# Long cross attention: queries of the first batches beside tile 9 of the running attention, peaks of batch 0 as 24 half steps beside its tiles 13 to 18

## What is computed

```python
q = _rope(q, T_q)          # 16 heads of 8, from x after the layer norm
k = _rope(k, T_k)          # 1500 context tokens
attn = jnp.einsum('bhqd,bhkd->bhqk', q, k) * SCALE
attn = jax.nn.softmax(attn, axis=-1)
out = jnp.einsum('bhqk,bhkd->bhqd', attn, v)
return out @ Wo.T
```

## Time and profile before

| | us |
|---|---|
| median of 3 runs (1635.27 to 1635.96) | 1635.84 |
| the profiled execution | 1629.23 |
| its span | 1627.4 |
| TensorE busy | 1475.6 (91%) |
| VectorE busy | 1066.2 (66%) |
| ScalarE busy | 868.7 (53%) |
| GpSimd busy | 744.2 (46%) |

### The profile page before, as it was taken

How to read it: one execution, slowest core, us unless ns; L and a number is a source line. 1 busy time by engine, 2 the same in 40 slices (tenths; PEclk the granted TensorE clock), 3 DMA queues, 4 the chain that set the end, 5 groups by cost and what they waited for, 6 DMA issues and landing times.

```text
span 1627.4 us, 41073 instructions
## 1 busy us (share of the span) xinstructions
PE 1475.6 (91%) x17022; PEld 947.9 (58%) x17022; DVE 1066.2 (66%) x1723; ACT 868.7 (53%) x1783; POOL 744.2 (46%) x670
## 2 busy tenths in 40 slices
PE   7879999999999799857699999999999999889998
PEld 4557888765444466525466666666666666555554
DVE  6885555433342377686588888888888888634554
ACT  3432333345654233315577777777777777743333
POOL 6773111100000057767488777778777776000000
PEclk9879999989999799968899999999999999989999
DMA  4003000041210420245555555464654654403320
GB/s 120 2 1 107 2 2 2 2 128 45 78 39 13 86 60 23 45 98 103 128 129 130 120 125 130 121 132 118 135 127 124 125 130 110 111 1 93 68 57 14
DMA packets 62539, 129.54 MB, mean 80 GB/s; under 512 B 15793, under 2 KB 38066, under 8 KB 59186
## 3 DMA queue, kind: packets, MB, share of 16 engines
q1 hardware_dynamic: 62354, 126.92, 33.5%
HBM read 100.22 MB, written 26.67 MB: 78 GB/s over the span
## 4 chain that ended last, share of the span: by engine, by line
PE 33%; POOL 11%; ACT 8%; issue 2%; DVE 2%; DMA 1%; SPq 0%; ACTq 0%; POOLq 0%; DVEq 0%
PE ps L1724 7%; POOL ARENA L1928 7%; PE ps L865 7%; PE ps L1708 5%; POOL ARENA L1934 4%; PE ps L877 3%; PE ps L1671 3%; ACT ARENA L1878 3%; PE ps L1662 2%; ACT ARENA L1856 2%; PE ps L1685 2%; ACT ARENA L1869 1%; ACT ARENA L1862 1%; PE ps L1733 1%; DVE ARENA L1798 1%
## 5 line engine op out<-in xcount | busy, mean ns | idle before, releaser
L1798 DVE TENSOR_REDUCE ARENA<-ps 112x2 f32<-112x1000 f32 x384 | 456.7, 1198 | 118.0 <-PE ps L1685 115.1
L1878 ACT ACTIVATE ARENA<-ps 125x448 f32<-125x448 f32 x768 | 378.4, 549 | 127.9 <-PE ps L1708 127.0
L1928 POOL TENSOR_TENSOR ARENA<-ARENA 64x500 f32<-64x500 f32 x192 | 264.8, 1379 | 104.4 <-ACT ARENA L1856 85.9
L107 POOL TENSOR_TENSOR rs<-rs,mhalf 128x1 f32<-128x1 f32 x96 | 57.7, 602 | 363.5 <-DVE rs L102 363.2
L865 PE MATMUL ps<-XT,ARENA 128*128 128x448 f32 x544 | 219.9, 549 | 0.0
L1708 PEld LDWEIGHTS ps<-ARENA 64*125 64x125 bf16 x3072 | 122.5, 134 | 133.3 <-ACT ARENA L1878 70.3
L1708 PE MATMUL ps<-ARENA 64*125 64x112 bf16 x3072 | 168.9, 228 | 20.0 <-ACT ARENA L1878 18.8
L1724 PE MATMUL ps<-ARENA 125*17 125x112 f32 x6144 | 184.9, 260 | 0.0
L865 PEld LDWEIGHTS ps<-XT,ARENA 128*128 128x128 f32 x544 | 104.6, 194 | 99.1 <-issue 98.7
L877 PE MATMUL ps<-ARENA 128*128 128x448 f32 x400 | 161.6, 539 | 0.0
L1685 PE MATMUL ps<-ARENA 64*112 64x500 bf16 x768 | 152.7, 387 | 9.0 <-DVE ARENA L1798 8.9
(11 more groups left out here) (228 smaller groups left out, 2106.2 us busy)
## 6 DMA issues: line engine op xcount, KB each, us to landing
ARENA<-key_parts SPq DMA_DIRECT2D x192, 187.5 KB, 4.1
ARENA<-in_ctxT SPq DMA_DIRECT2D x96, 250.0 KB, 3.8
key_parts<-ARENA SPq DMA_DIRECT2D x64, 375.0 KB, 2.7
ARENA<-token_weights SPq DMA_DIRECT2D x32, 512.0 KB, 5.6
ARENA<-in_L_ffn_W SPq DMA_DIRECT2D x1, 2048.0 KB, 8.8
ARENA<-query_parts SPq DMA_DIRECT2D x6, 192.0 KB, 6.0
ARENA<-in_c_ones SPq DMA_DIRECT2D x2, 562.5 KB, 14.7
ARENA<-in_L_attn_a SPq DMA_DIRECT2D x2, 512.0 KB, 5.3
```

Of the source, the lines that this page charges most:

```text
L1798: e.tensor_reduce(mxp[0:112, b % 2, 2 * g:2 * g + 2, ch], ps[0:112, b1:b1 + 2, 0:500], AX, ALU.max) \
L1878: e.activation(Pb[0:KT, n % NP_, 448 * h:448 * h + 448], ps[0:KT, b1[h], 0:448], ACT.Exp, bias=0.0, scale=1.0).then_inc(exped.sem, 1)
L1928: e.tensor_tensor(T2[r:r + 64, :], T0[64 - r:128 - r, n % 2, :], sin[64 - r:128 - r, sl], ALU.mult) \
```

## The change

Five things are changed.

1. Query 0 moves from tile 17 to tile 9, queries 1 and 2 from 18 and 19 to 17 and 18. They stand at the end of a tile, behind `output`. Query 0 uses bank 2 for both of its products, one after the other; each of the two matmuls now has its own signal.
2. The masks of batches 0, 1 and 2 move to tiles 12, 13 and 14 on GpSimd.
3. The twelve peaks of batch 0 become 24 half steps: one matmul of 64x112 by 500 into bank 2 and one reduce of 500 each. Half step k = 4 (t - 13) + i stands at place i of tile t, for t from 13 to 18. On TensorE the places are behind `project`, behind `running`, behind `turn` and behind `output`; on VectorE behind the product of values, behind the sum, behind the statistics and behind the early steps. Each matmul waits for the reduce of the half step before it; the first waits for the six stacks of batch 0's keys and for the mask.
4. `order()` has no peaks of batch 0; its `shift` comes right behind `clear`, `halve` to `full` behind two key matmuls. Of batch 2, the high and low parts of chunks 1 and 2, the writes and the stacks move from before the first score into the scores steps 0 to 2 of batch 0.
5. `Q0` and `mxp` are laid out ahead of what is allocated behind the first arena's part.

```diff
+                    half = stages[4].parts["half_pe"]
+                    half(e, w, t, 0)
                     if 1 <= t <= NT:
                         running(t - 1)
-                    stages[4].parts["early_pe"](e, w, t)
+                    half(e, w, t, 1)
+                    stages[4].parts["early_pe"](e, w, t, ("keys", "values"))
                     if t >= 4:
                         ln_turn(e, w, 4, t - 4, X_BANK, free)
                     if 2 <= t <= NT + 1:
                         turn(t - 2)
+                    half(e, w, t, 2)
                     if 3 <= t <= NT + 2:
                         output(t - 3)
+                    half(e, w, t, 3)
+                    stages[4].parts["early_pe"](e, w, t, ("query",))
...
+                    half = stages[4].parts["half_dve"]
+                    half(e, w, t, 0)
...
+                    half(e, w, t, 1)
                     u = t - 3
                     if 0 <= u < NT:
                         w.wait_ge(*projected(u + 1))
                         e.tensor_tensor(XR[:, u, :], ps[:, X_BANK, 0:128], XR[:, u, :], ALU.add).then_inc(joined.sem, 1)
                         w.wait_ge(*joined(u + 1))
                         ln_stats(e, w, 4, u)
+                    half(e, w, t, 2)
                     stages[4].parts["early_dve"](e, w, t)
+                    half(e, w, t, 3)
...
+                    for ch in (1, 2):
+                        f[ch - 1] += [("high", 2, ch), ("low", 2, ch)]
+                    f[2] += [("write", 2, 0), ("write", 2, 1)] + [("stack", 2, i) for i in range(6)]
...
-                yield from (("clear", 0), ("mask", 0), ("mask", 1), ("keys", 2, 0), ("keys", 2, 1))
-                for k in range(12):
-                    yield ("peak", 0, k)
+                yield from (("clear", 0), ("shift", 0), ("keys", 2, 0), ("keys", 2, 1), ("halve", 0), ("rest", 0), ("full", 0))
+                for k in range(6):
+                    yield ("peak", 1, k)
                     if k in (1, 3, 5):
                         yield ("blend", 2, k // 2)
                     if k == 1:
                         yield ("keys", 2, 2)
-                    if k in (6, 9):
-                        yield ("high", 2, k // 3 - 2)
-                        yield ("low", 2, k // 3 - 2)
-                yield from (("shift", 0), ("halve", 0), ("rest", 0), ("full", 0), ("mask", 2), ("high", 2, 2), ("low", 2, 2))
-                yield from (("write", 2, 0), ("write", 2, 1))
-                for i in range(6):
-                    yield ("stack", 2, i)
-                for k in range(6):
-                    yield ("peak", 1, k)
+                yield from (("high", 2, 0), ("low", 2, 0))
...
-                if 17 <= t <= 19:
-                    f.append(("query", t - 17))
+                if t == 9 or 17 <= t <= 18:
+                    f.append(("query", max(t - 16, 0)))
+                if 12 <= t <= 14:
+                    f.append(("mask", t - 12))
...
+            def half_of(t, i):
+
+                k = 4 * (t - 13) + i
+                return k if 0 <= k < 24 else None
+
+            def half_pe(e, w, t, i):
+                k = half_of(t, i)
+                if k is not None:
+                    g, ch = divmod(k // 2, 3)
+                    r = slice(64 * (k % 2), 64 * (k % 2) + 64)
+                    w.wait_ge(*ks_of(0))
+                    w.wait_ge(*masked(1))
+                    w.wait_ge(*free[2])
+                    e.matmul(ps[0:112, 2, 0:500], Q0[r, 0, g].rearrange("p j s -> p (j s)"),
+                             KS[0][r, g, 500 * ch:500 * ch + 500], start=True, stop=True).then_inc(half_mm.sem, 1)
+                    free[2] = half_peak(k + 1)
+
+            def half_dve(e, w, t, i):
+                k = half_of(t, i)
+                if k is not None:
+                    g, ch = divmod(k // 2, 3)
+                    x = 2 * g + k % 2
+                    w.wait_ge(*half_mm(k + 1))
+                    e.tensor_reduce(mxp[0:112, 0, x, ch:ch + 1], ps[0:112, 2, 0:500], AX, ALU.max).then_inc(half_peak.sem, 1)
...
-                    w.wait_ge(*peaked(12 * b + 12))
+                    w.wait_ge(*(peaked(12 * b) if b else half_peak(24)))
```

## The result

The changed kernel takes 1672.76 us (median of 4 runs, 1668.19 to 1681.3) against 1635.9 for the kernel before, a ratio of 1.0242 with a 95% interval of 1.0201 to 1.0282 (as estimated from all runs; the quotient of the two medians is 1.0225). Run once more in a later group it gave 1669.14 us against 1636.05, ratio 1.0203 [1.0167, 1.0239]. It is slower, by some 33 to 37 us; the forecast was 1657, the range 1643 to 1674.

The account below looks back on a forecast made before the run. It took the tail as a serial chain of half matmuls and VectorE reduces, and the head as bound by GpSimd. Terms: 25.4 late, -6.5 from the head, +2 clock, total +20.9 on 1635.84, giving 1657 us, range 1643 to 1674.

Parts of the forecast that it names:

- query at tile 9: At tile 9, the moved query makes TensorE late, mostly absorbed by VectorE's 2.57 us hole: +1.7 us, bounds 0.7 and 3.7.
- first half's wait: In tile 13, TensorE's first half matmul waits for batch 0's key stacks to land 9.0 us after issue: +9.2 us.
- tile 14: Tile 14's operations and half steps run in series, 11.9 us against 8.82 before: +3.1 us.
- to the end of output 13: Tiles 15 and 16 up to output 13 take 20.2 us against 17.9 before: +2.4 us.
- to the end of output 15: Tiles 17 and 18 with queries and half steps take 7.7 and 11.7 us, against 13.2 in all before: +6.2 us.
- to GpSimd's first sine: From the last output to batch 2's first sine product, one query fewer and earlier masks: about 9.6 us against 10.6, -1.0.
- the head gives back: In the cross attention's head, GpSimd's chain sets the pace and regains its 6.84 us wait: -6.5 us, bounds 0 and 16.
- clock: The pause at the first half step lowers TensorE's granted clock to 1.2 GHz for matmuls behind it: +2 us.
- third rival: Waits in tiles 13 to 18 keep TensorE's clock low: up to 26 us, some 16 likely, 1673; 13 in 100.
- second rival: VectorE and TensorE set the head's pace, not GpSimd, so all 16 us of peaks come back: +11, 1647; 17 in 100.
- The first and the last rival: First: halves vanish in the holes, 1622 or 1629, 7 in 100; last: costs and gains meet, +2.7, 3 in 100.

Follow-up runs that it names:

- x_warmtail: Changed kernel with useless small matmuls filling nearly all TensorE waits at the halves, including more in the last three tiles; 1655.6 us, ratio 1.013.
- b_query: Kernel before with only the queries and masks moved as the change does, the peaks left in the head; 1633.7 us, ratio 0.9999.
- x_noh: Changed kernel without its 24 half steps, batch 0's peaks left out and its maxima zeros; 1632.9 us, ratio 0.9986 to the kernel before.
- x_mm: Changed kernel with all half matmuls kept but every reduce except the last left out; 1640.7 us, ratio 1.0047 to the kernel before.
- b_key3: Kernel before with batch 3's first keys and their blend moved ahead among batch 1's first six peaks; 1632.8 us, ratio 1.0007.
- b_fetch: Kernel before with one DMA, the third part of batch 5's context, fetched a step earlier; 1624.6 us, ratio 0.9966.
- b_qk3: Kernel before with queries and masks moved as in the change and batch 3's first keys and blend earlier; 1633.6 us, ratio 1.0003.
- x_warmall: Changed kernel with 36 dummy matmuls ahead of the first half and seven ahead of each tile's fourth half; 1659.4 us, ratio 1.0133.
- x_fetch: Changed kernel with batch 3's context fetch listed at tile 14 instead of 12, which left the program the same; 1672.0 us, ratio 1.0224.

## Why the prediction was wrong

The sign and the mechanism were right; 1657 was 16 us short, at the edge of the range. By its own steps, with the changed kernel's own times:

| step | forecast | measured |
|---|---|---|
| query at tile 9 | +1.7 | +1.8; -0.4 in the second trace |
| first half's wait | +9.2 | +9.05 (8.89 idle) |
| rest of tile 13 | +3.8 | +6.3 |
| tile 14 | +3.1 | +3.6 |
| to the end of output 13 | +2.4 | +6.4 |
| to the end of output 15 | +6.2 | +13.3 |
| to GpSimd's first sine | -1.0 | +0.7 |
| sum | +25.4 | +41.1 (39.8 in the second trace) |
| the head gives back | -6.5 | -4.1 (-3.0) |
| clock | +2 | in the rows above |
| total | +20.9 | +37.0 (+36.8) |

The second trace stands 2.3 us lower in each sum for its first tile (see above); with that added it has 42.1 at the sine, and +1.9 for the query.

**The step that failed is the clock's +2.** With nearly all waits filled, x_warmtail comes to GpSimd's first sine 28.9 us late; the changed kernel's second and third traces, whose first tile ran like its own, come to it 39.8 and 38.6 us late. So the clock's term is some 10 us, not 2; that is 8 of the 16 that were missing. I had argued from the old tail, 0.92 with 16.6 of 26 us busy, that the new tiles would hold the clock, and for tiles 14 and 15 they mostly did (0.94). Where I was wrong is the last three tiles: 0.76, then 0.57. The third rival had the mechanism. That it had the time too, 1673, is luck: it put 16 us on a forecast that already held 2, while of the 16 that were missing only 8 are the clock's; the rest lies in the terms below. The Trainium skill (TensorE: Matmul & The Clock Gate, section "HAM oscillation — how this bites in real kernels"), which tells of a loop whose every round starts slow since it holds a wait, agrees with the last tiles and not with tiles 14 and 15; I should have given this rival more than 13 in 100.

**The chain was 5.8 us short even at full clock.** x_warmtail with its first tile's 2.3 us is 31.2 us late at the sine, where the sum had 25.4. Summing in series was right, and each piece somewhat too small: 10.0 us from the first half to the next projection (forecast 9.3), 12.4 for tile 14 (11.9), 2.0 too little up to the end of output 13, 20.1 from there to the end of output 15 (19.4), 1.7 too little ahead of the sine. That the moved queries cost the tail 5.6 us even without halves (b_query) was no term of its own; how much of the 5.8 it is, no run tells. With 8 for the clock and 2.4 for the head this makes up the 16.1 us between +20.9 and +37.0.

**The other terms.** The wait for the stacks was forecast to 0.2 us from the landing of that very transfer. That the alternation of half matmul and reduce makes a chain is confirmed three times over: without the reduces 28 us go, with them doubled 13 come, with a second bank 4 to 9 go.

**The head.** -6.5 was right in that the peaks don't set the head (the second rival's 16 us fell with x_noh) and somewhat too large: the changed kernel gets 3.0 to 4.2 us back in its three traces, x_noh and x_mm 4.4 and 4.5. GpSimd's rest of 6.84 us went, but one of 4.77 came for the cosine product. That GpSimd's row is what sets the head, as I had it, is not shown: b_key3 only moved its rest, and b_fetch took 6.5 us off by a DMA alone. I had asked what is late next and answered the stack of batch 2's keys; it was VectorE's blend, which the change's order puts behind batch 1's first peaks.

The first and the last rival are refuted: no kernel with reduces in the tiles is faster than before, and costs and gains did not meet.

**Left open.** Why the medians of b_query and b_qk3 don't show the 5.5 us of their traces (their lowest times are 4.6 and 2.1 us above the lowest of before). And why x_warmall's median is 11 us better than its own part says; its four runs don't decide it.

## What to carry to other kernels

Work that is slotted into the "free" time of two engines through one buffer ties them together: count it as a chain of matmul, reduce, matmul, not as busy time. Before moving work out of a stage, look in the chain of waits whether that work is what the stage hangs on; here a DMA one place too late in a queue was worth more than twelve peak steps moved. And where a change turns TensorE's full stretches into stretches with a rest in each step, give the halved clock a term of its own, by doubling the matmuls of the last, emptiest tiles. Before trusting a test, look in its trace whether the edit moved what it was meant to move; x_fetch moved nothing.

## What the runs showed of the hardware

Around the one long rest, 9 us, the granted clock was 0.78, and back at 0.94 in the next stretch. It stayed down only in the last tiles, with several rests of 0.8 to 3.3 us each: 0.76, then 0.57 (changed kernel's stretches above). Tiles 14 and 15 have rests of 0.5 to 1.7 us too and kept 0.94, so the runs give no rule. Filling the rests with matmuls of 0.23 us brought it to 0.97 to 1.00 and made the kernel some 10 us shorter by the traces, though TensorE then did more work.

Executions differ over code that is the same in all runs. The time to the attention's first projection is 555.2 to 563.3 us in the twenty traces (556.7 and 563.1 for the same kernel), and from the last full queries to the end it is 206.9 to 216.9. The four slowest ends, 216.4 us and more, are those in which the last batch's scores (21 us) had a granted clock of 0.53 to 0.58; in the others it was 0.84 or more. The own part leaves both out; over three traces of one program it was 37.0, 36.8 and 34.4 us.

The last of batch 0's six stacks landed 8.9 to 9.1 us after its issue with three context loads right behind, the last of batch 1's 8.4 to 9.0 us with none. The six land one after another: 3.6, 4.8, 5.9, 6.9, 8.0 and 8.9 us after their issues in the changed kernel, which issues them 0.4 to 0.5 us apart.
